# Score and maximum products on row tiles of the TensorE array, with dense rings of queries and keys

## The chip, the cores and the metric

One core of a Trainium2 chip runs the whole program. The metric is device time in microseconds (us); the program was timed three times.

## What is computed

For each of 8 blocks of 512 tokens with 256 channels, two gated layers. `xn` is the layer norm of `x`; each layer adds attention times SiLU of a feed-forward net:

```python
x = x + L0_attn(xn) * silu(L0_ffn(xn))      # 16 query heads of 16 channels on 4 key heads, ALiBi-like bias
xn = layernorm(x)
x = x + L1_attn(xn) * silu(L1_ffn(xn))      # 32 query heads of 8 channels, in pairs: a0 - lambda * a1
# both: scores = q @ k.T * scale (+ bias), causal; softmax; @ v; @ Wo
# L0_ffn: silu(x W1) * (x W3), Hadamard transform, W2 ; L1_ffn: shared expert plus top 2 of 8 experts
```

## The kernel before

The attention of a block is cut into **units** of four query heads: units 0 to 3 are layer 0, units 4 to 11 layer 1. A loop (`nc.Fori`) runs over the 8 blocks. Each engine has its instructions in an order written out by hand, with semaphores between engines; nothing is reordered by a planner.

Products of queries and keys use high and low parts stacked along the contraction, so that q and k have 48 rows in layer 0 (three times 16) and 24 in layer 1. The SyncE queue loads them from images in memory into two-slot rings, `qring` and `kring` (`ring_load`, L302 to L309). A ring has 128 rows. In layer 0 rows 0 to 47 hold the heads' 48 rows. In layer 1 the four heads of a unit lie at rows 0, 32, 64 and 96 of `kring`, and in `qring` each head has its own full-width plane that is zero outside its own 32 rows: a product over all 128 rows then gives that head's scores. The last row (`MROW`, row 127) holds ones in the keys and, in the queries, minus each query's maximum score, so that the score product (`pe_score_pack`, L410) subtracts it.

The maxima come one unit ahead: `pe_max_pack` (L387) multiplies queries by keys for unit u + 1, a product with an identity and a causal mask in bf16 (L391) adds the mask to the diagonal block, `dve_maxima` (L645) reduces each row. `pe_max_turn` (L397) transposes the 16 maxima of each token, ScalarE copies them (L543), and `max_row` (L323) writes them by DMA into row 127 of the ring. Two PSUM banks (`MX`) take the maximum products and two (`SC`) the scores; pack n waits until the reader of pack n - 2 is done.

A unit has 11 **packs**: keys tile 0 for each of 4 heads (512 columns), tile 1 for each (384), tile 2 for two heads at once (512), twice, and tile 3 for all four (512). On TensorE pack i is: score product of unit u, maximum product or products of unit u + 1, mask product; in layer 0 also an up product of the feed-forward net between them (`pe_up_between`, L338). ScalarE takes the exponent of each score pack (L554), GpSimd cuts the diagonal blocks (L1358; in layer 0 L665 and L668, with L656 on VectorE), and `pe_pv` (L425) multiplies by the values: the four heads write 17 columns each, at output partitions 0, 32, 64 and 96. In layer 1 the value product of tile 0 (pv0) stands after pack 5, that of tile 1 (pv1) after pack 10, then come the turn of the maxima (L397), twelve up products, and the value products of tiles 2 and 3 together.

Units 4 to 10 have score and maximum packs side by side; so have units 0 to 2. Units 3 and 11 have scores alone. The maxima of unit 4 are made in the front of layer 1 among up products, those of unit 0 of the next block at the end of the iteration among down products (`pe_down`, L486). The order on TensorE in a unit:

```python
for i in range(PACKS):
    pe_score_pack(pe, u, i)
    if more:
        pe_max_pack(pe, u + 1, i)
...
    if i == (7, 5)[layer_of(u)]:
        pe_pv(pe, u, 0)
...
pe_pv(pe, u, 1)
```

## Time and profile before

| what | value |
|---|---|
| three runs | 2509.87, 2512.74 and 2505.23 us, median 2509.87 us |
| profiled execution, first to last instruction (its span) | 2511.7 us |
| TensorE (PE) busy | 2154.0 us, 86% of the span |
| weight loads (PEld) | 1470.1 us, 59% |
| VectorE (DVE) | 1466.3 us, 58% |
| ScalarE (ACT) | 926.7 us, 37% |
| GpSimd (POOL) | 750.2 us, 30% |
| mean granted TensorE clock | 0.943 of full speed |

The profiled execution has no separate time beside its span; the span lies inside the range of the three runs, 1.8 us above their median. Busy time is the union of the instructions of an engine. The ends of matmuls are modelled, and include the way through the array, so start-to-start distances say more than durations. In a timeline row `x4` stands for four instructions merged; what stands in brackets is the idle time of the engine before the row, and who ended it.

### The profile page before, as it was taken

How to read it: one execution, taken by the hardware profiler on the slowest of the kernel's cores; microseconds unless marked ns; L12 is line 12 of the kernel's file. 1: busy time of each engine (PE TensorE's matmuls, PEld its weight loads, DVE VectorE, ACT ScalarE, POOL GpSimd, SP SyncE). 2: the span in 40 equal slices, each digit the busy share in tenths (PEclk: the TensorE clock that was granted, in tenths of full speed). 3: DMA queues.
4: the chain of work that ended last, by engine and by line, in shares of the span. 5: the costliest groups of instructions: out<-in, count | busy, mean ns of one | idle time of the engine just before them, and what ended most of it. 6: DMA issues, size and time to landing. Idle time of an engine off the chain costs nothing. (4 is left out here: it accounts for less than half of the span.)

```text
span 2511.7 us, 34684 instructions
## 1 busy us (share of the span) xinstructions
PE 2154.0 (86%) x12379; PEld 1470.1 (59%) x12476; DVE 1466.3 (58%) x2657; ACT 926.7 (37%) x1826; POOL 750.2 (30%) x916
## 2 busy tenths in 40 slices
PE   2379997899978999799988999789997899979998
PEld 1247565565656656475564756557565665646556
DVE  4475664656565664656647566465655566465564
ACT  2242541425323352324514245142532335233352
POOL 2342331423223331323314233142322333132331
PEclk7599998999989999899999999899998999989999
DMA  6723322253311532215232342224331253221522
GB/s 216 247 62 127 114 92 49 64 158 91 90 42 52 178 88 77 55 57 171 73 91 59 107 138 80 56 68 146 104 90 36 58 177 87 80 55 48 172 81 81
DMA packets 108131, 245.94 MB, mean 98 GB/s; under 512 B 17188, under 2 KB 27956, under 8 KB 107676
## 3 DMA queue, kind: packets, MB, share of 16 engines
q1 hardware_dynamic: 93676, 199.46, 26.5%
q0 software_dynamic: 14256, 43.94, 6.0%
q8 instruction: 111, 1.82, 0.3%
q14 instruction: 88, 0.72, 0.1%
HBM read 182.75 MB, written 59.79 MB: 97 GB/s over the span
## 5 line engine op out<-in xcount | busy, mean ns | idle before, releaser
L645 DVE TENSOR_REDUCE nmax<-bank 128x1 f32<-128x512 f32 (+3 forms) x1067 | 661.4, 639 | 457.5 <-PE bank L391 445.9
L554 ACT ACTIVATE probs<-bank 128x512 f32<-128x512 f32 (+1 forms) x1056 | 578.0, 560 | 515.5 <-PE bank L410 490.1
L338 PE MATMUL bank<-xnT,upring 128*128 128x512 f32 (+1 forms) x2220 | 626.7, 405 | 22.2 <-DMA upring<-up_img 22.2
L410 PE MATMUL bank<-qring,kring 128*128 128x512 f32 (+1 forms) x1056 | 493.1, 470 | 91.1 <-issue 47.4
L387 PE MATMUL bank<-kring,qring 127*128 127x512 f32 (+3 forms) x1552 | 480.0, 362 | 87.7 <-DMA kring<-k_img 50.1
L338 PEld LDWEIGHTS bank<-xnT,upring 128*128 128x128 f32 x2220 | 402.6, 193 | 98.8 <-issue 38.3
L387 PEld LDWEIGHTS bank<-kring,qring 127*128 127x128 f32 x1552 | 287.2, 202 | 162.3 <-DVE nmax L645 79.3
L410 PEld LDWEIGHTS bank<-qring,kring 128*128 128x128 f32 x1056 | 216.7, 206 | 216.8 <-issue 108.5
L486 PE MATMUL bank<-wdown,hbuf 128*128 128x256 f32 x1408 | 342.0, 393 | 0.0
L425 PE MATMUL bank<-probs,v 128*17 128x512 f32 (+3 forms) x3072 | 271.6, 449 | 64.9 <-DVE probs L656 40.4
L1358 POOL TENSOR_SCALAR_AFFINE_SELECT probs<-probs 128x512 f32<-128x512 f32 x256 | 162.5, 635 | 518.0 <-ACT probs L554 516.4
L486 PEld LDWEIGHTS bank<-wdown,hbuf 128*128 128x128 f32 x1408 | 268.0, 197 | 34.8 <-issue 1.7
L665 POOL TENSOR_SCALAR_AFFINE_SELECT probs<-probs 128x256 f32<-128x256 f32 x128 | 67.5, 527 | 663.9 <-ACT probs L554 663.8
L673 DVE SCALAR_TENSOR_TENSOR hbuf<-tb,bank 128x512 f32<-128x512 f32 x176 | 120.5, 685 | 224.3 <-ACT tb L564 223.4
L391 PE MATMUL bank<-causal_bf,ident_bf 128*128 128x128 bf16 (+1 forms) x970 | 245.2, 253 | 0.0
L656 DVE SCALAR_TENSOR_TENSOR probs<-probs,shared 128x512 f32<-128x512 f32 (+3 forms) x256 | 210.6, 848 | 49.7 <-ACT probs L554 48.9
L668 POOL TENSOR_TENSOR probs<-probs,shared 128x1024 f32<-128x1024 f32 (+3 forms) x128 | 211.8, 1654 | 10.7
L391 PEld LDWEIGHTS bank<-causal_bf,ident_bf 128*128 128x128 bf16 x1067 | 108.6, 102 | 178.6 <-issue 152.4
L564 ACT ACTIVATE tb<-bank 128x512 f32<-128x512 f32 x176 | 105.3, 599 | 151.3 <-PE bank L338 151.3
L425 PEld LDWEIGHTS bank<-probs,v 128*17 128x17 f32 x3072 | 61.4, 96 | 148.8 <-issue 56.0
L681 DVE SCALAR_TENSOR_TENSOR hbuf<-hbuf,bank 128x512 f32<-128x512 f32 x176 | 120.4, 684 | 33.0 <-PE bank L338 21.6
L1317 POOL TENSOR_TENSOR hbuf<-hbuf,gring 128x512 f32<-128x512 f32 x88 | 112.7, 1280 | 48.4 <-DMA gring<-gate_img 40.3
(118 smaller groups left out, 1540.1 us busy)
## 6 DMA issues: line engine op xcount, KB each, us to landing
upring<-up_img SPq DMA_DIRECT2D x179, 512.0 KB, 4.0
q_img<-probs SPq DMA_DIRECT2D x102, 256.0 KB, 3.9
qring<-q_img SPq DMA_DIRECT2D x256, 64.0 KB, 1.9
kring<-k_img SPq DMA_DIRECT2D x64, 256.0 KB, 3.1
qring<-q_img SPq DMA_DIRECT2D x34, 384.0 KB, 5.3
k_img<-probs SPq DMA_DIRECT2D x48, 256.0 KB, 4.9
up_img<-hbuf POOLq DMA_DIRECT2D x22, 512.0 KB, 4.6
gring<-gate_img POOLq DMA_DIRECT2D x32, 256.0 KB, 3.7
```

The costliest lines, as they stand in the source:

```text
L338: last = nc.tensor.matmul(out_ap, part_a(a, pa, k), part_b(b, pb, k), start=(n == 0), stop=(n == len(steps) - 1))
L387: nc.tensor.matmul(bk[:, (g - g0) * w:(g - g0 + 1) * w], qring[l][0:MROW, s, g, qt * P:(qt + 1) * P], kring[l][0:MROW, s, 0:w], start=True ...
L391: nc.tensor.matmul(diag, ident_bf[:], causal_bf[:, 0:heads, :], start=False, stop=True, skip_group_check=True).then_inc(s_mp[k], 1)
L410: nc.tensor.matmul(SC[n % 2][:, 0:heads * w].rearrange("p (g n) -> p g n", g=heads), kring[l][:, s, kt * P:(kt + 1) * P], qring[l][:, s, g ...
L425: last = nc.tensor.matmul(PV[32 * g:32 * g + DV + 1, kt * P:T], v[l][:, kt, hv, :], probs[:, kt % 2, g, 0:T - P * kt], start=(kt == 0), st ...
L486: last = nc.tensor.matmul(FB[tt // 2][:, (tt % 2) * C:(tt % 2 + 1) * C], hbuf[:, j, tt * P:(tt + 1) * P], wdown[l][:, j, :], start=(j == 0 ...
L554: nc.scalar.activation(probs[:, kt % 2, g0:g0 + heads, 0:w], SC[n % 2][:, 0:heads * w].rearrange("p (g n) -> p g n", g=heads), ACT.Exp, sc ...
L645: nc.vector.tensor_reduce(nmax[:, u % 2, g0:g0 + heads, qt], MX[n % 2][:, 0:heads * w].rearrange("p (g n) -> p g n", g=heads), AX.X, ALU.m ...
L656: nc.vector.scalar_tensor_tensor(pr, pr, BIG, estrip[:, g, 0:w], ALU.min, ALU.mult).then_inc(s_pm, 1)
L668: nc.gpsimd.tensor_tensor(pr[:, :, 0:w], pr[:, :, 0:w], estrip[:, 2:4, 0:w], ALU.mult).then_inc(s_pm2, 1)
L673: nc.vector.scalar_tensor_tensor(hbuf[:, layer_tile(j)[1], :], tb[:], 1.0, FB[0][:], ALU.add, ALU.mult).then_inc(s_gu, 1)
L1358: nc.gpsimd.affine_select(pr, pr, [[0, G4], [1, P]], ALU.is_ge, 0.0, base=0, channel_multiplier=-1).then_inc(s_pm, 1)
```

## The change

Nothing is computed otherwise; products move to other rows of the array.

- **Layer 0**: `qring[0]` and `kring[0]` lose their slot dimension. Slot 0 lies at rows 0 to 48, slot 1 at rows 64 to 112; the maximum sits in row 48 of the slot. A score product of unit u uses the 49 rows of its slot, a maximum product of unit u + 1 the 48 of the other one.
- **Layer 1**: `qring[1]` is one plane, head g at rows 32 g to 32 g + 24, without the zeros. A product takes the 24 or 25 rows of one head, so packs hold one head each: 12 steps rather than 11 packs. Steps 0 to 3 are key tile 0 (512 columns), steps 4 to 7 tiles 1 and 3 of one head (384 and 128 columns, two products in one bank), steps 8 to 11 tile 2 (256). The maximum product beside the score of head g is that of head (g + 2) mod 4. Steps 4 to 7 take two reductions each on VectorE.
- The value products of layer 1 come in three steps: pv0 after step 6, pv1 (tiles 1 and 3) after step 10 and so ahead of step 11, tile 2 last.
- Ring loads of layer 1 are one DMA of 128 rows for the queries in place of four of 32 rows. Three memsets of rings in the set-up go.
- The mask product (128 rows of the array) and all up, down and value products stay as they were.

```diff
-MROW = P - 1
 PACKS = 11
+STEPS_OF = (11, 12)
+HROWS = 32
+KROWS = (48, 24)
 
 SCORE_PACKS = [(0, g, 1) for g in range(4)] + [(1, g, 1) for g in range(4)] + [(2, 0, 2), (2, 2, 2), (3, 0, 4)]
 MAX_PACKS = [(3, g, 1) for g in range(4)] + [(2, g, 1) for g in range(4)] + [(1, 0, 2), (1, 2, 2), (0, 0, 4)]
 PACKS_TO = (4, 8, 10, 11)
+
+PARTS_1 = (((0, 0),), ((1, 0), (3, 384)), ((2, 0),))
+
+MAX_PARTS_1 = (((3, 0),), ((2, 0), (0, 384)), ((1, 0),))
...
+def score_base(u):
+    return sum(STEPS_OF[layer_of(i)] for i in range(u))
+
+
+def pv_base(u):
+    return sum((NT, len(PARTS_1))[layer_of(i)] for i in range(u))
+
+
+def max_base(u):
+    return sum(STEPS_OF[layer_of(i)] for i in range(1, u))
+
+
+def max_head(i):
+    return (i + 2) % G4
...
-        qring = [sb("qring0", [P, 2, G4, T], F32R), sb("qring1", [P, 2, G4, T], F32R)]
-        kring = [sb("kring0", [P, 2, T], F32R), sb("kring1", [P, 2, T], F32R)]
+        qring = [sb("qring0", [P, G4, T], F32R), sb("qring1", [P, 2, T], F32R)]
+        kring = [sb("kring0", [P, T], F32R), sb("kring1", [P, 2, T], F32R)]
...
-                sp.dma_start(qring[0][0:48, s, :, :].bitcast(F32),
+                sp.dma_start(qring[0][64 * s:64 * s + 48, :, :].bitcast(F32),
                              q_img[0][4 * w:4 * w + 4].rearrange("g r n -> r g n")).then_inc(done, 16)
-                sp.dma_start(kring[0][0:48, s, :].bitcast(F32), k_img[0][w]).then_inc(done, 16)
+                sp.dma_start(kring[0][64 * s:64 * s + 48, :].bitcast(F32), k_img[0][w]).then_inc(done, 16)
-                for g in range(G4):
-                    sp.dma_start(qring[1][32 * g:32 * g + 32, s, g, :].bitcast(F32), q_img[1][4 * w + g]).then_inc(done, 16)
+                sp.dma_start(qring[1][:, s, :].bitcast(F32),
+                             q_img[1][4 * w:4 * w + 4].rearrange("g r n -> (g r) n")).then_inc(done, 16)
...
-            sp.dma_start(qring[layer_of(u)][MROW:MROW + 1, u % 2, :, :].rearrange("a g (t n) -> a (g t) n", t=NT)
-                         .bitcast(F32), mneg[:].bitcast(F32)).then_inc(s_mrow[k], 16)
+            if layer_of(u) == 0:
+                row = 64 * (u % 2) + KROWS[0]
+                sp.dma_start(qring[0][row:row + 1, :, :].rearrange("a g (t n) -> a (g t) n", t=NT)
+                             .bitcast(F32), mneg[:].bitcast(F32)).then_inc(s_mrow[k], 16)
+            else:
+                sp.dma_start(qring[1][KROWS[1]:P:HROWS, u % 2, :].bitcast(F32), mneg[:].bitcast(F32)).then_inc(s_mrow[k], 16)
...
-            n = PACKS * before + i
-            qt, g0, heads = MAX_PACKS[i]
-            w = P * (qt + 1)
+            n = max_base(u) + i
             if n >= 2:
                 pe.wait_ge(s_mr[k], n - 1)
             bk = MX[n % 2]
-            for g in range(g0, g0 + heads):
-                nc.tensor.matmul(bk[:, (g - g0) * w:(g - g0 + 1) * w], qring[l][0:MROW, s, g, qt * P:(qt + 1) * P],
-                                 kring[l][0:MROW, s, 0:w], start=True, stop=True)
-
-            diag = bk[:, 0:heads * w].rearrange("p (g n) -> p g n", g=heads)[:, :, qt * P:w]
-            nc.tensor.matmul(diag, ident_bf[:], causal_bf[:, 0:heads, :], start=False, stop=True,
-                             skip_group_check=True).then_inc(s_mp[k], 1)
+            if l == 0:
+                qt, g0, heads = MAX_PACKS[i]
+                w = P * (qt + 1)
+                rows = slice(64 * s, 64 * s + KROWS[0])
+                for g in range(g0, g0 + heads):
+                    nc.tensor.matmul(bk[:, (g - g0) * w:(g - g0 + 1) * w], qring[0][rows, g, qt * P:(qt + 1) * P],
+                                     kring[0][rows, 0:w], start=True, stop=True)
+                diag = bk[:, 0:heads * w].rearrange("p (g n) -> p g n", g=heads)[:, :, qt * P:w]
+                last = nc.tensor.matmul(diag, ident_bf[:], causal_bf[:, 0:heads, :], start=False, stop=True,
+                                        skip_group_check=True)
+            else:
+
+                rows = slice(HROWS * max_head(i), HROWS * max_head(i) + KROWS[1])
+                parts = MAX_PARTS_1[i // G4]
+                for qt, at in parts:
+                    nc.tensor.matmul(bk[:, at:at + P * (qt + 1)], qring[1][rows, s, qt * P:(qt + 1) * P],
+                                     kring[1][rows, s, 0:P * (qt + 1)], start=True, stop=True)
+                diag = parts[0][0] * P
+                last = nc.tensor.matmul(bk[:, diag:diag + len(parts) * P], ident_bf[:], causal_bf[:, 0:len(parts), :],
+                                        start=False, stop=True, skip_group_check=True)
+            last.then_inc(s_mp[k], 1)
...
-
-            nc.tensor.matmul(SC[n % 2][:, 0:heads * w].rearrange("p (g n) -> p g n", g=heads),
-                             kring[l][:, s, kt * P:(kt + 1) * P],
-                             qring[l][:, s, g0:g0 + heads, kt * P:T], start=True, stop=True).then_inc(s_sc, 1)
-
-        def pe_pv(pe, u, kt):
+            if l == 0:
+                kt, g0, heads = SCORE_PACKS[i]
+                w = T - P * kt
+                rows = slice(64 * s, 64 * s + KROWS[0] + 1)
+                last = nc.tensor.matmul(SC[n % 2][:, 0:heads * w].rearrange("p (g n) -> p g n", g=heads),
+                                        kring[0][rows, kt * P:(kt + 1) * P],
+                                        qring[0][rows, g0:g0 + heads, kt * P:T], start=True, stop=True)
+            else:
+                g = i % G4
+                rows = slice(HROWS * g, HROWS * g + KROWS[1] + 1)
+                for kt, at in PARTS_1[i // G4]:
+                    last = nc.tensor.matmul(SC[n % 2][:, at:at + T - P * kt], kring[1][rows, s, kt * P:(kt + 1) * P],
+                                            qring[1][rows, s, kt * P:T], start=True, stop=True)
+            last.then_inc(s_sc, 1)
...
-                pe.wait_ge(s_pm, 8 * U0[1] + 4 * (u - U0[1]) + kt + 1)
+                pe.wait_ge(s_pm, 8 * U0[1] + NT * (u - U0[1]) + (1, 3, 4)[step])
+                parts = PARTS_1[step]
-            for g in range(G4):
-                hv = u if l == 0 else 2 * (u - U0[1]) + g // 2
-                last = nc.tensor.matmul(PV[32 * g:32 * g + DV + 1, kt * P:T], v[l][:, kt, hv, :],
-                                        probs[:, kt % 2, g, 0:T - P * kt], start=(kt == 0),
-                                        stop=(kt == NT - 1), skip_group_check=True)
+            for kt, at in parts:
+                for g in range(G4):
+                    hv = u if l == 0 else 2 * (u - U0[1]) + g // 2
+                    last = nc.tensor.matmul(PV[32 * g:32 * g + DV + 1, kt * P:T], v[l][:, kt, hv, :],
+                                            probs[:, n % 2, g, at:at + T - P * kt], start=(kt == 0),
+                                            stop=(kt == (3, 2)[l]), skip_group_check=True)
...
+                step, g0, heads = i // G4, i % G4, 1
+                w = (T, T, 2 * P)[step]
...
+            if layer_of(u) == 0:
+                qt, g0, heads = MAX_PACKS[i]
+                last = nc.vector.tensor_reduce(nmax[:, u % 2, g0:g0 + heads, qt],
+                                               MX[n % 2][:, 0:heads * P * (qt + 1)].rearrange("p (g n) -> p g n", g=heads),
+                                               AX.X, ALU.max, negate=True)
+            else:
+                for qt, at in MAX_PARTS_1[i // G4]:
+                    last = nc.vector.tensor_reduce(nmax[:, u % 2, max_head(i), qt:qt + 1],
+                                                   MX[n % 2][:, at:at + P * (qt + 1)], AX.X, ALU.max, negate=True)
+            last.then_inc(s_mr[k], 1)
...
-                sp.wait_ge(s_qz, 1)
-                nc.gpsimd.memset(qring[0][:].rearrange("p a g n -> p (a g n)").bitcast(F32), 0.0)
-                nc.gpsimd.memset(kring[0][:].rearrange("p a n -> p (a n)").bitcast(F32), 0.0).then_inc(s_qz, 1)
-                    if t == UP_EARLY + 6:
-                        nc.vector.memset(qring[1][:].rearrange("p a g n -> p (a g n)").bitcast(F32), 0.0)
...
-                            if i == (7, 5)[layer_of(u)]:
+                            if i == (7, 6)[layer_of(u)]:
                                 pe_pv(pe, u, 0)
+                            if layer_of(u) == 1 and i == 10:
+                                pe_pv(pe, u, 1)
-                        pe_pv(pe, u, 1)
+                        if layer_of(u) == 0:
+                            pe_pv(pe, u, 1)
...
-                        for kt in range(NT):
-                            pool.wait_ge(s_exp, PACKS * u + PACKS_TO[kt])
-                            pr = probs[:, kt % 2, :, 0:P]
+                        for step in range(len(PARTS_1)):
+                            pool.wait_ge(s_exp, score_base(u) + G4 * (step + 1))
+                            pr = probs[:, (pv_base(u) + step) % 2, :, :]
+                            for _, at in PARTS_1[step]:
+                                diag = pr[:, :, at:at + P]
+                                nc.gpsimd.affine_select(diag, diag, [[0, G4], [1, P]], ALU.is_ge, 0.0, base=0,
+                                                        channel_multiplier=-1).then_inc(s_pm, 1)
```

**Order, TensorE, end of a layer-1 unit.** `L410` (now `L455`) is the score product, `L387` (`L424`) the maximum product, `L391` (`L427`) the mask product, `L425` (`L474`) the value product, `L397` (`L434`) the turn of the maxima and `L338` (`L363`) the up products. Before, from pack 10 on:

```order
L410 MATMUL bank<-qring,kring 128x512
L387 MATMUL bank<-kring,qring 128x128 x4
L391 MATMUL bank<-causal_bf,ident_bf 128x512
L425 MATMUL bank<-probs,v 17x384 x4
L397 MATMUL bank<-ident,nmax 16x128
L338 MATMUL bank<-xnT,upring 128x512 x12
L425 MATMUL bank<-probs,v 17x256 x4
L425 MATMUL bank<-probs,v 17x128 x4
```

Now, from step 10 on:

```order
L455 MATMUL bank<-qring,kring 128x256
L424 MATMUL bank<-kring,qring 128x256
L427 MATMUL bank<-causal_bf,ident_bf 128x128
L474 MATMUL bank<-probs,v 17x384 x4
L474 MATMUL bank<-probs,v 17x128 x4
L455 MATMUL bank<-qring,kring 128x256
L424 MATMUL bank<-kring,qring 128x256
L427 MATMUL bank<-causal_bf,ident_bf 128x128
L434 MATMUL bank<-ident,nmax 16x128
L363 MATMUL bank<-xnT,upring 128x512 x12
L474 MATMUL bank<-probs,v 17x256 x4
```

The value product of tile 1 stood behind the last mask product; now it stands ahead of the last step, and takes tile 3 along, which had stood at the end of the unit.

**Order, VectorE, the same unit.** `L645` (now `L705`) reduces maxima, `L694` and `L701` (`L754`, `L761`) divide the outputs of the unit before. Before:

```order
L645 TENSOR_REDUCE nmax<-bank 128x1 x5
L694 RECIPROCAL rden<-bank 128x16
L701 TENSOR_TENSOR shared<-bank,rden 128x4x64
L645 TENSOR_REDUCE nmax<-bank 128x1 x3
L645 TENSOR_REDUCE nmax<-bank 128x2 x2
L645 TENSOR_REDUCE nmax<-bank 128x4
```

Now:

```order
L705 TENSOR_REDUCE nmax<-bank 128x1 x6
L754 RECIPROCAL rden<-bank 128x16
L761 TENSOR_TENSOR shared<-bank,rden 128x4x64
L705 TENSOR_REDUCE nmax<-bank 128x1 x10
```

Eleven reductions have become sixteen.

## Rows read from the trace of the kernel before

**Rows 1.** The page, part 1: busy time, share of the span, instructions of each engine.
```profile
PE 2154.0 (86%) x12379; PEld 1470.1 (59%) x12476; DVE 1466.3 (58%) x2657; ACT 926.7 (37%) x1826; POOL 750.2 (30%) x916
```

**Rows 2.** TensorE matmuls of one layer-1 unit (timeline: start us, us, engine, line).
```profile
932.64 0.50 PE L410 MATMUL bank<-qring,kring 128*128 128x512 f32 x1
...
933.21 0.23 PE L391 MATMUL bank<-causal_bf,ident_bf 128*128 128x128 bf16 x1
...
934.23 0.51 PE L387 MATMUL bank<-kring,qring 127*128 127x512 f32 x1
934.57 0.23 PE L391 MATMUL bank<-causal_bf,ident_bf 128*128 128x128 bf16 x1
...
936.69 1.05 PE L425 MATMUL bank<-probs,v 128*17 128x512 f32 x8
937.67 0.44 PE L410 MATMUL bank<-qring,kring 128*128 128x384 f32 x1
...
942.20 0.27 PE L397 MATMUL bank<-ident,nmax 128*16 128x128 f32 x1
...
945.22 0.84 PE L425 MATMUL bank<-probs,v 128*17 128x256 f32 x16
946.00 0.50 PE L410 MATMUL bank<-qring,kring 128*128 128x512 f32 x1
946.33 0.39 PE L338 MATMUL bank<-xnT,upring 128*128 128x512 f32 x1
946.56 0.40 PE L410 MATMUL bank<-qring,kring 128*128 128x512 f32 x1
```

**Rows 3.** VectorE in the same unit (timeline).
```profile
933.48 2.65 DVE L645 TENSOR_REDUCE nmax<-bank 128x1 f32<-128x512 f32 x4 [0.77 <-PE bank L391]
...
936.79 0.25 DVE L694 RECIPROCAL rden<-bank 128x16 f32<-128x16 f32 x1
937.07 0.42 DVE L701 TENSOR_TENSOR shared<-bank,rden 128x256 f32<-128x256 f32 x1
...
938.40 1.04 DVE L645 TENSOR_REDUCE nmax<-bank 128x1 f32<-128x384 f32 x2 [0.44 <-PE bank L391]
...
941.36 0.69 DVE L645 TENSOR_REDUCE nmax<-bank 128x4 f32<-128x512 f32 x1 [0.39 <-PE bank L391]
```

**Rows 4.** GpSimd in the same unit (timeline).
```profile
935.90 0.64 POOL L1358 TENSOR_SCALAR_AFFINE_SELECT probs<-probs 128x512 f32<-128x512 f32 x1 [5.33 <-ACT probs L554]
936.50 1.28 POOL L1317 TENSOR_TENSOR hbuf<-hbuf,gring 128x512 f32<-128x512 f32 x1
```

**Rows 5.** Reductions of layer maxima by form (groups of VectorE instructions).
```profile
L645 DVE TENSOR_REDUCE nmax<-bank 128x1 f32<-128x512 f32 x388 | 257.3, 688 | 278.8 <-PE bank L391 270.1
L645 DVE TENSOR_REDUCE nmax<-bank 128x1 f32<-128x384 f32 x388 | 208.8, 553 | 101.6 <-PE bank L391 100.3
```

**Rows 6.** TensorE waiting in layer 0 (waits: us in total, times, longest).
```profile
PE bank L425 <- DVE probs L656: 40.4, 32, 1.8
```

**Rows 7.** VectorE in layer 0, unit 1: reductions of its first four packs (timeline).
```profile
1038.38 3.14 DVE L645 TENSOR_REDUCE nmax<-bank 128x1 f32<-128x512 f32 x4 [0.78 <-PE bank L391]
```

**Rows 8.** The chain of waits late in the last iteration.
```profile
2495.55 1.35 PE bank L486 x6
```

**Rows 9.** Set-up: VectorE and ScalarE (timeline).
```profile
9.37 4.78 DVE L602 TENSOR_SCALAR xn<-xin,mv,rstd 128x256 f32<-128x256 f32 x2 [1.14 <-POOL rstd L611]
...
14.05 1.67 ACT L884 CAST wqk<-probs 128x640 fp32r<-128x640 f32 x2 [11.96 <-DMA probs<-in_w_gate]
```

**Rows 10.** Stretches by window: start:end, us, busy us of each engine (count), clock, DMA.
```profile
932.60:946.00 13.40, 13.13 (x92) 7.95 (x88) 8.61 (x17) 7.14 (x14) 4.39 (x6) 1.00 0.10 21
...
1021.60:1025.00 3.40, 1.38 (x8) 0.73 (x7) 3.40 (x3) 1.22 (x3) 3.28 (x3) 1.00 0.00 0
...
1055.70:1059.00 3.30, 1.00 (x7) 0.70 (x6) 0.20 (x2) 1.45 (x3) 0.00 (x0) 1.00 0.59 170
```

**Rows 11.** Twelve up products at the lower clock, set-up (timeline of TensorE).
```profile
67.07 5.47 PE L338 MATMUL bank<-xnT,upring 128*128 128x512 f32 x12
```

80 lines of the change are left out of this document (40 added, 40 removed).

## The prediction

> **What bounds the kernel now.** The page comes first: TensorE is busy 86% of the span, VectorE 58% [rows 1]. That share counts the way through the array, so I read a single layer-1 unit instead, of which seven in each of the 8 iterations have score and maximum products side by side (units 4 to 10): 56 in all. In the window of one such unit TensorE is busy 13.13 of 13.40 us, VectorE 8.61 [rows 10]. The timeline shows that this is closer than it looks [rows 2, 3]. The unit starts at 932.64, its maxima are turned at 942.20, 9.56 us later, and the next unit starts at 946.00, after 13.36 us. VectorE's four first reductions run in one piece, 2.65 us for four of 0.69 [rows 3, 5]. With two banks a loop binds both engines: a reduction ends (933.48 + 0.69), 0.06 later the maximum product of the pack after next starts (934.23), 0.34 later its mask product (934.57), and 0.27 later the reduction of that bank (933.21 to 933.48). That is 0.69 + 0.06 + 0.34 + 0.27 = 1.36 us for two packs, 0.68 for one. The score product is outside this loop: it is over while TensorE waits for the bank. So in these packs what the change hides is already hidden.
>
> **What a switch of tiles costs.** No row of before has a row tile. The nearest are the value products, whose four heads write at four places of the array: eight matmuls of 512 columns take 0.98 us start to start (936.69, next score product 937.67), where one such matmul after another takes 0.23 (946.33 to 946.56), so eight would take 1.84 [rows 2]. Tiles do run side by side, and I take pairs on different rows to do so too. Going back from the tiles costs: the first full matmul after them holds the array 0.33 (946.00 to 946.33) and not 0.23. I take 0.10 us a switch back to the whole array, and nothing for going into tiles. The bounds are 0, if only tiles across columns pay, and 0.20, if both directions do. The mask product still uses all 128 rows, so each step switches. The Trainium skill has a rule for this, "TensorEngine Tiling (Array Packing)", Tiling Modes, Key Properties: a change of tiling mode (not of tile) drains TensorE; it gives no price, the 0.10 of the trace agrees with it, and without it the sum would be that of rivals 2 or 3.
>
> **The change, part by part.**
>
> *Layer 1, paired units.* First reduction: 0.84 after the unit's start now; the score product's 0.23 goes beside the maximum product, a switch comes: 0.71. Steps 0 to 3: the loop is 1.36 + 0.10, so 0.73 a step, 2.92 together: 3.63. Steps 4 to 7 have two reductions each. A 384-wide one takes 0.55, a 512-wide one 0.69 [rows 5], 0.14 per 128 columns, so a 128-wide one 0.27; two of 0.55 in a row take 1.04 [rows 3], so pairs overlap by 0.07: 0.75. The products have 512 columns as before (0.34), the mask 256 (+0.05): 0.75 + 0.06 + 0.34 + 0.10 + 0.05 + 0.27 = 1.57, 0.79 a step, 3.15 for four; with 0.67 of dividing between them (0.25 + 0.42) [rows 3] that gives 7.45. Steps 8 and 9 are 256 wide: reduction 0.41, product 0.23, (0.41 + 0.06 + 0.23 + 0.10 + 0.27) / 2 = 0.54 each, so the reduction of step 10 starts at 8.53 and its mask product stood at 8.26. **Here the order bites.** Now pv1 runs while VectorE reduces the last pack, and the turn follows. In the new order pv1 comes first: 0.98 as pv0 [rows 2], because it has 512 columns, from 8.33 to 9.31. Then come the last pair (0.33, after tiles), a switch (0.10), 0.27, the reduction 0.41, and 0.15 to the turn (941.36 + 0.69 to 942.20) [rows 2, 3]: 10.57 rather than 9.56, +1.01. Behind the up products only tile 2 is left: of the 0.78 now, 0.57 is columns (0.21 being the way out), a third of it goes: -0.19. **+0.82 a unit, 56 units: +46 us.** Between pv0 and pv1 GpSimd has a mask (0.64) and weighs a tile (1.28) [rows 4], then two masks: with score 7 done by 6 that ends before 8.3, so it hides. Bounds: switch 0: 0 us for 56 units; 0.20: +1.7 a unit, +95.
>
> *Layer 0, paired units.* Units 1 and 2 have an up product behind each pack; a pack takes 0.82, since four reductions that wait for it span 3.14 us, (3.14 - 0.69) / 3 [rows 7]. The pair saves 0.23, and mask and up products are full-array, so a pack pays one switch and its score's weight load is exposed (another 0.10): nearly nothing left, and the unit then waits for VectorE's distances (40.4 us over the run) [rows 6]. I take 0 for units 1 and 2. Unit 0 runs at the lower clock, where 512 columns take twice as long: its first reduction starts 0.4 earlier, VectorE is the bound from then on: 8 x -0.4 = **-3 us**. Bounds 0 and -37 (second rival).
>
> *Maxima and scores without a partner.* 12 steps in front of layer 1 and 11 packs at the end of the iteration stand among full-array products, where the down products are on the chain that ended last [rows 8]. Nothing runs beside them, each pays a switch: 23 x 0.10 x 8 = **+18 us**. Unit 3 (8 packs) and unit 11 (6 steps) alternate scores with up products; half of them wait for ScalarE anyway: 14 x 0.10 x 8 / 2 = **+6 us**. Bounds 0 and +50.
>
> *Rings.* One query DMA in place of four: the row of maxima is written later than the ring load is issued, so SyncE gains nothing that TensorE sees. Bytes are the same. *Set-up:* a memset on GpSimd goes, which held VectorE (4.78 us for an operation of 0.7), but ScalarE waited for the weights until 14.05 anyway [rows 9]; the memset on VectorE may give back up to 3: **-2 us**, once.
>
> **Sum:** 46 - 3 + 18 + 6 - 2 = +65 us. The profiled execution has 2511.7 us, the three runs a median of 2510; on the median: **2575 us**.
>
> **Rivals.**
>
> 1. *The clock falls.* TensorE now idles more in the steps. In this trace the lower level (1.2 GHz rather than 2.4) followed stretches in which it was busy 1.38 of 3.40 us and 1.00 of 3.30, and in the unit of the same view it stayed at full speed [rows 10]. Against it: between pv0 and the up products few gaps of such a length arise; for it: two products that ran one behind the other now run at once, with nothing in the place of the second. If the up products of half the units ran at the lower level, 12 of them take 5.47 us [rows 11] and not the 3.0 between turn and value product [rows 2]: 28 x 2.5 = +70, 2645 us.
> 2. *Pairs pay, switches don't* (the other side). Decided by the switch: at about 0 layer 1 comes out even (above), and in layer 0 the scores leave TensorE's path: units 1 and 2 save 4 x 0.23 + 3 x 0.17 = 1.4 each, unit 0 at the lower clock 4 x 0.43 = 1.7, so 4.6 x 8 = 37, with 2 of set-up: 2470 us. For it: tiles that run side by side [rows 2]; against: the 0.10 there. The skill's "TensorE: Matmul & The Clock Gate", Part 3, measured four row tiles of 512 columns at 3.07 times one after the other; this kernel never has more than two in a pair, and no row here shows row tiles.
> 3. *No change.* As 2, but VectorE's waits take what layer 0 gains: 2505 us.
> 4. *Row tiles do not run side by side.* Then the first and the last step of a unit lose 0.23 each: 56 x 0.5 = +28, 2603 us; inside the range of the forecast.
>
> **How the numbers follow.** About 0.3% (7.5 us) is what a measurement of this kernel tells from no change. Forecast with rival 4: 0.44, own range 2530 to 2610. Clock: 0.16. No change: 0.16. Pairs pay: 0.24, since my loop prices a form of reduction and a switch that no row shows. The range leaves out about half of rival 2 below and half of rival 1 above: 2480 to 2640. Faster 0.24, within 0.3% 0.16, slower 0.60.
>
> **What would show it.** Right: in a layer-1 unit the score and maximum products start within 0.15 us of each other, the turn comes 10.2 to 10.9 us after the start, the unit takes about 14.2; a mask product after a 512-wide pair starts 0.4 or more after it; maxima among down products hold TensorE longer. Wrong: the pack steps of layer 1 go below 0.6 us, or the turn comes before 9.6; granted clock in layer 1 below 1.00 would be rival 1; layer-0 units shorter by over 1 us would be rival 2.

## The result and the profile after

The changed kernel takes 2916.25 us (median of four runs, 2910.39 to 2924.71) against 2507.55 us before (four runs, 2504.87 to 2512.74): a ratio of 1.1635, 95% interval 1.1608 to 1.1663. It is slower by 409 us. The forecast was 2575 us, within 2480 to 2640: the direction was right and the size six times too small.

The profiled execution spans 2917.3 us. The page of the changed kernel, busy time and granted clock by slices (tenths of full speed), against [rows 1]:

```profile
PE 2662.9 (91%) x12860; PEld 1602.1 (55%) x12860; DVE 1460.5 (50%) x2976; ACT 942.6 (32%) x1890; POOL 739.0 (25%) x914
...
PEclk7588787877879769696688876888788876969679
```

VectorE's busy time hardly moved (1466 to 1461 us) although it has 16 reductions a layer-1 unit rather than 11. TensorE's grew by 509 us, and the mean granted clock fell from 0.943 to 0.788. The next view shows where. Each window is one layer-1 unit, from the turn of its maxima to the next turn, with busy time of each engine, then the clock:

```profile
core 0: us, PE busy (x) PEld busy (x) DVE busy (x) ACT busy (x) POOL busy (x), PEclk, DMA share, GB/s
995.42:1012.86 17.44, 16.83 (x93) 9.40 (x94) 8.99 (x20) 7.25 (x15) 4.83 (x7) 0.79 0.23 77
1012.86:1032.00 19.14, 18.53 (x94) 9.81 (x94) 9.06 (x20) 7.33 (x15) 4.36 (x6) 0.68 0.23 70
1032.00:1053.02 21.02, 20.42 (x93) 10.61 (x94) 9.14 (x20) 7.34 (x15) 4.79 (x7) 0.58 0.20 63
```

Before, such a unit took 13.40 us at a clock of 1.00 [rows 10]. Now it takes 17.4, 19.1 or 21.0 us, and the length follows the clock. Yet TensorE is busy 96 or 97% of each window. In before the lower level came right behind the two stretches of [rows 10] in which TensorE was busy for less than half of the time:

```profile
1025.00:1031.80 6.80, 5.46 (x21) 3.29 (x22) 4.34 (x7) 1.19 (x2) 1.68 (x3) 0.50 0.00 0
...
1059.00:1062.60 3.60, 3.60 (x12) 1.92 (x11) 1.90 (x3) 1.94 (x5) 0.00 (x0) 0.53 0.00 0
```

In the changed kernel there is no such stretch: all that is idle in each of the three windows is 0.6 us.

The timeline of TensorE in the changed kernel, one step at each level of the clock, and what follows the last maxima:

```profile
1047.40 0.58 PE L455 MATMUL bank<-qring,kring 25*128 25x256 f32 x1
1047.41 0.57 PE L424 MATMUL bank<-kring,qring 24*128 24x256 f32 x1
1047.92 0.29 PE L427 MATMUL bank<-causal_bf,ident_bf 128*128 128x128 bf16 x1
...
1058.77 0.49 PE L455 MATMUL bank<-qring,kring 25*128 25x512 f32 x1
1058.77 0.49 PE L424 MATMUL bank<-kring,qring 24*128 24x512 f32 x1
1059.19 0.23 PE L427 MATMUL bank<-causal_bf,ident_bf 128*128 128x128 bf16 x1
1059.35 0.50 PE L455 MATMUL bank<-qring,kring 25*128 25x512 f32 x1
...
1070.38 0.37 PE L434 MATMUL bank<-ident,nmax 128*16 128x128 f32 x1 [0.61 <-DVE nmax L705]
1070.50 5.01 PE L363 MATMUL bank<-xnT,upring 128*128 128x512 f32 x12
```

Score and maximum products start together (1058.77 and 1058.77), so the row tiles do run side by side. (In the whole trace about four of five pairs start within 0.02 us, the others mostly 0.2 to 0.4 us apart, which fits a wait for a bank.) A step at full clock takes 0.58 us (1058.77 to 1059.35). After the turn twelve up products take 5.01 us, where at full clock they take 3.0.

The starts of the 97 turns of maxima in both traces cut the run into stretches. Means over the iterations, in us, with the clock in brackets:

| stretch between turns | before | after | difference over the run |
|---|---|---|---|
| unit 0 (seven of them) | 27.5 (0.73) | 25.0 (0.63) | -18 |
| unit 1 | 18.2 (1.00) | 20.7 (0.81) | +20 |
| unit 2 | 21.7 (0.93) | 27.1 (0.65) | +43 |
| unit 3, layer 0's end, front of layer 1 | 70.7 (0.99) | 74.9 (0.96) | +33 |
| units 4 to 10, each | 14.1 (0.99) | 19.1 (0.70) | +281 (56 units) |
| unit 11 and the iteration's end | 62.8 (0.96) | 68.6 (0.93) | +46 |

The sum is +405, and the spans differ by 2917.3 - 2511.7 = 405.6. The layer-1 units hold seven tenths of it.

### The profile page after: what moved, and what is told of

Same layout as the page of the kernel before. It is cut to its first block and busy times, and to the rows that moved or that the text cites. A ratio compares the mean times of both kernels' runs of the same rounds, so it can differ in the third digit from the quotient of the medians.

```text
span 2917.3 us, 35801 instructions
## 1 busy us (share of the span) xinstructions
PE 2662.9 (91%) x12860; PEld 1602.1 (55%) x12860; DVE 1460.5 (50%) x2976; ACT 942.6 (32%) x1890; POOL 739.0 (25%) x914
## 5 line engine op out<-in xcount | busy, mean ns | idle before, releaser
L609 ACT ACTIVATE probs<-bank 128x512 f32<-128x512 f32 (+2 forms) x1120 | 593.3, 538 | 724.6 <-PE bank L455 404.3
L363 PE MATMUL bank<-xnT,upring 128*128 128x512 f32 (+1 forms) x2220 | 805.7, 497 | 1.4 <-DVE hbuf L733 1.0
L705 DVE TENSOR_REDUCE nmax<-bank 128x1 f32<-128x512 f32 (+3 forms) x1024 | 461.4, 487 | 331.8 <-PE bank L427 326.6
L363 PEld LDWEIGHTS bank<-xnT,upring 128*128 128x128 f32 x2220 | 508.7, 244 | 126.0 <-issue 27.4
L424 PE MATMUL bank<-kring,qring 24*128 24x512 f32 (+3 forms) x1024 | 417.4, 451 | 0.1
L455 PE MATMUL bank<-qring,kring 25*128 25x128 f32 (+3 forms) x1024 | 411.5, 449 | 0.7
L474 PE MATMUL bank<-probs,v 128*17 128x512 f32 (+3 forms) x3072 | 365.9, 584 | 4.4 <-DVE probs L716 3.3
L455 PEld LDWEIGHTS bank<-qring,kring 25*128 25x128 f32 x1024 | 204.8, 224 | 213.4 <-issue 145.3
L448 PE MATMUL bank<-qring,kring 49*128 49x512 f32 (+1 forms) x352 | 215.4, 616 | 80.3 <-issue 46.4
L414 PE MATMUL bank<-kring,qring 48*128 48x256 f32 (+3 forms) x528 | 238.0, 508 | 55.3 <-DMA kring<-k_img 43.9
L424 PEld LDWEIGHTS bank<-kring,qring 24*128 24x128 f32 x1024 | 207.9, 226 | 42.0 <-issue 25.1
L427 PE MATMUL bank<-causal_bf,ident_bf 128*128 128x128 bf16 (+1 forms) x768 | 212.6, 277 | 0.0
```

What stands on the lines that cost most here:

```text
L363: last = nc.tensor.matmul(out_ap, part_a(a, pa, k), part_b(b, pb, k), start=(n == 0), stop=(n == len(steps) - 1))
L414: nc.tensor.matmul(bk[:, (g - g0) * w:(g - g0 + 1) * w], qring[0][rows, g, qt * P:(qt + 1) * P], kring[0][rows, 0:w], start=True, stop=True)
L424: nc.tensor.matmul(bk[:, at:at + P * (qt + 1)], qring[1][rows, s, qt * P:(qt + 1) * P], kring[1][rows, s, 0:P * (qt + 1)], start=True, sto ...
L427: last = nc.tensor.matmul(bk[:, diag:diag + len(parts) * P], ident_bf[:], causal_bf[:, 0:len(parts), :], start=False, stop=True, skip_grou ...
L448: last = nc.tensor.matmul(SC[n % 2][:, 0:heads * w].rearrange("p (g n) -> p g n", g=heads), kring[0][rows, kt * P:(kt + 1) * P], qring[0][ ...
L455: last = nc.tensor.matmul(SC[n % 2][:, at:at + T - P * kt], kring[1][rows, s, kt * P:(kt + 1) * P], qring[1][rows, s, kt * P:T], start=Tru ...
```

## The experiments

The first theory was that TensorE's clock falls because the products use few rows of the array, however busy the engine is. Its rivals: the new order of steps does it; or two products at once do it, since they fill less time than two in a row. All ratios are to the kernel before, timed beside it. Each kernel was run twice, those of experiment 11 six and twelve times.

**1. Layer 1 back on 128 rows, the new order kept.**

```diff
-rows = slice(HROWS * g, HROWS * g + KROWS[1] + 1)
+rows = slice(0, P)             # qring[1] has its zeros and its plane for each head again
...
-rows = slice(HROWS * max_head(i), HROWS * max_head(i) + KROWS[1])
+rows = slice(0, P - 1)
```

> The change with its layer-1 score and maximum products on all 128 rows again (zero-padded query ring); its twelve steps, its sixteen reductions and its early second value product stay, and so do the layer-0 row tiles. If the products on few rows make the clock fall (first theory): granted clock 1.00 in nearly all layer-1 units, a unit of 14 to 15 us rather than 17.4 to 21.0, and 2560 to 2640 us in all. If the new order of steps does it (rival): clock 0.58 to 0.79 in the units as in the change, over 2850 us.

Measured: 2661.54 us, ratio 1.0591 (1.0545 to 1.0637). Windows of two units, and the timeline around the start of the second:

```profile
941.73:956.78 15.05, 13.79 (x93) 8.80 (x94) 8.93 (x20) 7.27 (x15) 4.37 (x6) 1.00 0.32 89
956.78:971.93 15.15, 13.79 (x94) 8.80 (x94) 8.92 (x20) 7.28 (x15) 4.81 (x7) 1.00 0.29 87
```

```profile
941.73 0.27 PE L435 MATMUL bank<-ident,nmax 128*16 128x128 f32 x1 [0.61 <-DVE nmax L706]
...
945.86 0.47 PE L456 MATMUL bank<-qring,kring 128*128 128x512 f32 x1 [0.46 <-DMA qring<-mneg]
946.17 0.40 PE L425 MATMUL bank<-kring,qring 127*128 127x512 f32 x1
946.41 0.23 PE L428 MATMUL bank<-causal_bf,ident_bf 128*128 128x128 bf16 x1
946.45 0.48 PE L456 MATMUL bank<-qring,kring 128*128 128x512 f32 x1
...
956.78 0.27 PE L435 MATMUL bank<-ident,nmax 128*16 128x128 f32 x1 [0.61 <-DVE nmax L706]
```

The clock is back at 1.00 with order and reductions unchanged, so the order is not what lowers it. 255 us of the loss are gone (2916 to 2662). What stays is 1.7 us a unit over 13.4 (experiment 6). The total is 22 us above the expected range: the units take 15.0 to 15.2 us where nothing disturbs them and 15.9 on the mean of all 56 (before 14.1), and layer 0 keeps its own loss (experiment 4).

**2. The pair on the same rows.** The maximum product of head i beside the score product of head i:

```diff
 def max_head(i):
-    return (i + 2) % G4
+    return i % G4
```

> The change with the maximum product of each layer-1 step on the same rows as the score product beside it (head i mod 4 rather than two further), so the two cannot run at once. If the clock falls because a product on 25 rows counts little whatever runs beside it (first theory): the units stay at 0.58 to 0.79, the maximum product starts 0.1 to 0.25 us after the score product rather than 0.01, and the time is 2910 to 3000 us. If the clock falls because two products at once fill less time than two in a row (rival): it returns to 0.9 or more in the units, and the time falls to 2650 to 2800 us.

Measured: 3187.84 us, ratio 1.2685 (1.2601 to 1.2769), slower than expected. A window and a step at full clock:

```profile
1100.16:1125.05 24.89, 24.28 (x94) 14.03 (x94) 9.45 (x20) 7.43 (x15) 4.34 (x6) 0.57 0.19 54
```

```profile
1105.92 0.50 PE L455 MATMUL bank<-qring,kring 25*128 25x512 f32 x1
1106.27 0.40 PE L424 MATMUL bank<-kring,qring 24*128 24x512 f32 x1
1106.59 0.23 PE L427 MATMUL bank<-causal_bf,ident_bf 128*128 128x128 bf16 x1
```

The maximum product now starts 0.35 us after its neighbour, TensorE is busy 98% of the window, and the clock is lower still (0.57; on the mean of the 56 units 0.61, in the change 0.69). Running at once is therefore not what lowers it. Without it the program loses another 272 us; how much of that is the longer step and how much the clock was not taken apart.

**3 and 4. One layer alone.** The change in layer 1 alone; then in layer 0 alone, on the kernel before. The lines that differ are the change's own, for instance:

```diff
-rows = slice(64 * s, 64 * s + KROWS[0])       # 3: layer 0 as before
+rows = slice(0, P - 1)
...
-qring[l][0:MROW, s, g, qt * P:(qt + 1) * P]   # 4: layer 0 on row tiles
+qring[0][64 * s:64 * s + 48, g, qt * P:(qt + 1) * P]
```

> The change in layer 1 alone: layer 0 has its zero-padded 128-row products back. From the spans between turns I expect layer 1 to hold 56 x 5.6 us of the 409 and the rest of its part (unit 3 to 4, the end of the iteration): 2820 to 2870 us. If the low clock in layer 0 were what pulls layer 1 down, it would be under 2750.

> The kernel before with the row tiles of layer 0 alone (49 and 48 rows, base 0 and 64). If products on 49 rows lower the clock too: units 1 and 2 below 0.85 clock, 2540 to 2600 us. If only the 25-row tiles do (rival): clock as before, and, with score and maximum products side by side, 2470 to 2505 us.

Measured: layer 1 alone 2882.87 us, ratio 1.1472 (1.1356 to 1.1588); layer 0 alone 2547.32 us, 1.0136 (1.0096 to 1.0177). That is +371 and +35 us, together 406 of the 409, so the two parts add. The range for layer 1 was passed by 13 us. With layer 0 alone the clock is 0.87 in unit 1 and 0.68 in unit 2 on the mean (expected: both below 0.85), and 0.99 in the layer-1 units as in before.

**5. Tiles of 64 rows.** Two heads' rows a tile, the other head's query rows zero; still a pair at once:

```diff
-rows = slice(HROWS * g, HROWS * g + KROWS[1] + 1)
+rows = slice(64 * (g // 2), 64 * (g // 2) + 64)   # qring[1][rows, s, g % 2, ...]
```

> The change with the layer-1 row tiles made 64 rows high (two heads' rows, the other head's query rows zero), so a score and a maximum product still run at once, on 2 x 64 rows rather than 25 + 24. If the number of rows in use is what the clock goes by (first theory): 0.95 or more in the layer-1 units, a unit of 15.0 to 15.7 us, 2620 to 2700 us in all. If two products at once, or row tiles as such, make it fall (rival): clock 0.6 to 0.8 as in the change and 2850 us or more.

Measured: 2711.98 us, ratio 1.0816 (1.0674 to 1.0957), 12 us above the range. Units 6 to 10 at full clock, the pair starting together:

```profile
931.03:945.91 14.88, 13.98 (x93) 7.72 (x94) 8.98 (x20) 7.27 (x15) 4.84 (x7) 1.00 0.30 90
945.91:960.98 15.07, 14.03 (x93) 7.74 (x94) 8.99 (x20) 7.28 (x15) 4.37 (x6) 1.00 0.28 89
```

```profile
950.63 0.50 PE L455 MATMUL bank<-qring,kring 64*128 64x512 f32 x1
950.64 0.50 PE L424 MATMUL bank<-kring,qring 63*128 63x512 f32 x1
951.07 0.23 PE L427 MATMUL bank<-causal_bf,ident_bf 128*128 128x128 bf16 x1
951.23 0.50 PE L455 MATMUL bank<-qring,kring 64*128 64x512 f32 x1
```

So neither row tiles nor pairs need lower the clock: these units have the pairs and the changes between tiles and whole array of the change, with more rows in use. They do not hold it everywhere. Units 4 and 5 have 0.92 and 0.86 (experiment 1: 0.98 and 0.93), and the stretch from unit 3 to the front of layer 1, where maxima on 63 rows have no partner, has 0.94 and 76.9 us (experiment 1: 0.99 and 71.9). That stretch is the larger part of what this kernel loses against experiment 1.

This is also the clean price of a pair: at full clock a step of 512 columns takes 0.60 us on row tiles (950.63 to 951.23) and 0.59 on 128 rows (945.86 to 946.45). There the pair saves nothing; over a whole unit at full clock it saves 0.1 to 0.4 us (means of units 6 to 8 and 10: 14.8 to 15.0 against 15.1).

**6. The value product of tiles 1 and 3 back behind the last step**, on the kernel of experiment 1 and on the change itself:

```diff
-                            if layer_of(u) == 1 and i == 10:
-                                pe_pv(pe, u, 1)
...
-                        if layer_of(u) == 0:
-                            pe_pv(pe, u, 1)
+                        pe_pv(pe, u, 1)
```

> The kernel of the first run (128 rows in layer 1, new order) with the value product of tiles 1 and 3 back behind the last step, where VectorE's last reduction covers it. My forecast put +1.0 us of the order's cost in that move: the unit falls from 15.05 to 14.1 and the time from 2662 to about 2605. Rival: the sixteen reductions and the twelve steps themselves cost the 1.7 us over before's 13.38, and the unit stays at 14.7 or more, 2640 us or more.

> The change with only the value product of tiles 1 and 3 back behind the last step. With 128 rows this was worth 1.1 us a unit, 85 in all. If it is a wait of its own beside the clock: 1.0 to 2.0 us a unit less at the same clocks, 2800 to 2860 us. If the lower clock covers it (rival): over 2890 us.

Measured: 2576.86 us with 128 rows, ratio 1.0277 (1.0213 to 1.034), 28 us below what was expected; 2855.54 us on the change, 1.1402 (1.1356 to 1.1448), inside the range for a wait of its own beside the clock. One window of each:

```profile
911.08:924.97 13.89, 13.70 (x98) 8.73 (x95) 8.93 (x20) 7.27 (x15) 4.36 (x6) 1.00 0.35 97
```

```profile
1039.31:1057.62 18.31, 18.31 (x97) 9.62 (x93) 9.05 (x20) 7.33 (x15) 4.81 (x7) 0.69 0.22 72
```

At full clock the move alone cost 1.1 us a unit, and what is left over 13.38 is 0.6. On the change TensorE is busy for the whole window, and yet the clock is at 0.69, which is the lower level for six tenths of the time. The same order on 128 rows, busy 13.70 of 13.89 us, has 1.00.

**7. More work.** A useless product (bf16) on all 128 rows ahead of each layer-1 score product of the change, into the bank that the score product overwrites:

```diff
+nc.tensor.matmul(SC[n % 2][:, 0:512], ident_bf[:], causal_bf[:, 0:4, :], start=True, stop=True)
 rows = slice(HROWS * g, HROWS * g + KROWS[1] + 1)
```

> The change with one added product on all 128 rows, 512 columns, ahead of every layer-1 score product, into the bank that the score product then overwrites: useless work, 12 x 0.21 us a unit at the full clock. If too few rows in use make the clock fall (first theory): 0.95 or more in the units, about 15.4 + 2.5 = 17.9 us a unit rather than 19.1 on average, and 2820 to 2880 us: more work, less time. If the clock goes by something that full products do not mend (rival): 12 x 0.21 to 12 x 0.43 a unit on top, 3050 to 3200 us.

Measured: 2785.99 us, ratio 1.1111 (1.103 to 1.1192). Two windows, and a step:

```profile
973.48:989.97 16.49, 15.59 (x103) 7.56 (x106) 9.20 (x20) 7.44 (x15) 4.34 (x6) 1.00 0.25 81
989.97:1006.46 16.49, 15.59 (x103) 7.56 (x106) 9.20 (x20) 7.44 (x15) 4.79 (x7) 1.00 0.27 81
```

```profile
1001.83 0.38 PE L453 MATMUL bank<-causal_bf,ident_bf 128*128 128x512 bf16 x1
1002.13 0.38 PE L456 MATMUL bank<-qring,kring 25*128 25x256 f32 x1
1002.14 0.38 PE L424 MATMUL bank<-kring,qring 24*128 24x256 f32 x1
```

Twelve added products a unit make the unit 16.5 us long rather than 17.4 to 21.0, and the program 130 us faster than the change. The tiles, the pairs and the number of changes between tiles and whole array are those of the change, so none of them as such lowers the clock. It did better than expected (16.5, not 17.9 us): the unit is 1.6 us longer than the 14.9 of experiment 5, while twelve products at 0.21 us are 2.5. That part of the added work falls into waits is my reading, not tested.

**8. Both layers on 64 rows, the value product back.** Experiments 5 and 6 together, and layer 0 on tiles of 64 rows:

```diff
-rows = slice(64 * s, 64 * s + KROWS[0] + 1)
+rows = slice(64 * s, 64 * s + 64)
```

> Row tiles of 64 rows in both layers (zero padding to 64, the row of maxima in row 63 of its tile) and the value product of tiles 1 and 3 back behind the last step. If rows in use decide the clock: layer-1 units at 1.00 and 14.0 to 14.6 us, units 1 and 2 of layer 0 at 0.9 or more, 2530 to 2600 us. If layer-0 tiles of 64 rows still lower the clock where a product runs without a partner (rival): layer 0 as in the change, 2590 to 2640 us.

Measured: 2634.95 us, ratio 1.0508 (1.043 to 1.0586): the rival's range, and 58 us slower than the 128 rows of experiment 6. Units 6 to 8 and 10 take 14.0 to 14.2 us at 0.98 or 0.99, but units 4, 5 and 9 take 15.9, 17.1 and 16.0 at 0.92, 0.84 and 0.90, so 64 rows in pairs do not hold the full clock throughout. Unit 1 has 0.91, but unit 2 runs at a clock of 0.71 and the stretch from unit 3 to the front of layer 1, where maxima have no partner, takes 77.2 us.

**9. The mask products left out**, on the kernel of experiment 5, so that pair follows pair:

```diff
-last = nc.tensor.matmul(bk[:, diag:diag + len(parts) * P], ident_bf[:], causal_bf[:, 0:len(parts), :],
-                        start=False, stop=True, skip_group_check=True)
```

> The run with 64-row tiles in layer 1, without the causal mask product of the layer-1 maxima (the maximum is then taken over keys that the mask leaves out as well), so a pair is followed by a pair and nothing changes back to 128 rows between them. If the way back to the whole array costs about 0.2 us a step: from the start of a 512-wide pair to its reduction 0.48 us rather than 0.69, and 0.5 to 1.5 us less a unit, 2620 to 2690 us, VectorE's reductions being the bound. If the mask products are what still held the clock up (rival): clock under 0.9 in the units and over 2750 us.

Measured: 2685.28 us, ratio 1.0722 (1.0683 to 1.0762), inside the first range. A unit at full clock takes 14.2 to 14.4 us.

```profile
950.68 0.50 PE L452 MATMUL bank<-qring,kring 64*128 64x512 f32 x1 [0.31 <-DMA kring<-k_img]
950.69 0.50 PE L424 MATMUL bank<-kring,qring 63*128 63x512 f32 x1
951.02 0.39 PE L452 MATMUL bank<-qring,kring 64*128 64x512 f32 x1
```

A pair is followed by the next pair after 0.34 us, and by the mask product after 0.43 (950.64 to 951.07): going back to 128 rows costs about 0.09. From the mask product to the next pair 0.16 us pass (951.07 to 951.23), where on 128 rows it is 0.04 (946.41 to 946.45): going into the tiles costs 0.12. So a pair with its two changes takes 0.43 + 0.12 = 0.55 us, exactly as long as two products one behind the other on 128 rows (945.86 to 946.41). The clock of the 56 units is 0.91 on the mean, against 0.97 in experiment 5, and several fell to 0.7 to 0.9, so the full-height mask products did help to hold it; neither expectation had this alone.

**10. Layer 0: few rows, or waits?** First the filler of experiment 7 in layer 0 (512 columns, on the kernel of experiment 4), which did not settle it:

```diff
+if l == 0:
+    nc.tensor.matmul(SC[n % 2][:, 0:512], ident_bf[:], causal_bf[:, 0:4, :], start=True, stop=True)
```

> The run with layer-0 row tiles alone, and one useless product on all 128 rows, 512 columns, ahead of each layer-0 score product. If rows in use decide the clock in layer 0 too (first theory): 1.00 in units 1 and 2, which take about 20 and 22 us; the total is within 2530 to 2560 us, since 11 x 0.21 us a unit go back into it. If not (rival): clock 0.87 and 0.68 as without it, and 2570 to 2620 us.

Measured: 2589 us, ratio 1.0338 (1.028 to 1.0395), unit 1 at 0.96 and unit 2 at 0.75 of the clock. The clock rose by 0.07 to 0.09, short of the 1.00 of the first theory, and the time is in the rival's range: 42 us slower than without the added products. Then two kernels that take the causes apart: before with its layer-0 products on rows 0 to 48 alone, both slots on the same rows, so no pair; and pairs of 64 rows.

```diff
-kring[l][:, s, kt * P:(kt + 1) * P],
-qring[l][:, s, g0:g0 + heads, kt * P:T],
+kring[l][rows, s, kt * P:(kt + 1) * P],      # rows = slice(0, (49, P)[l])
+qring[l][rows, s, g0:g0 + heads, kt * P:T],
```

> The kernel before with its layer-0 products reading rows 0 to 48 and 0 to 47 alone (row of maxima in row 48), both units' rings at the same rows, so nothing can run side by side; layer 1 as before. If few rows in use lower the clock in layer 0 too (first theory): 0.9 or less in unit 1 and 0.75 or less in unit 2, 20 and 25 us or more, and 2540 to 2600 us. If it is the wait for VectorE behind a faster pair (rival): clock and times of units 1 and 2 as in before, 2500 to 2515 us.

> The run with layer-0 row tiles alone, padded to 64 rows with zeros, so a pair uses 127 rows. If few rows in use are the cause (first theory): unit 1 at 0.95 or more and under 18.2 us, unit 2 at 0.85 or more, 2480 to 2510 us. If a pair's short time and the waits behind it are the cause (rival): unit 2 stays at 0.75 or less and 24 us, 2520 to 2550 us.

Measured: 49 rows without a pair 2646.47 us, ratio 1.0566 (1.053 to 1.0601); pairs of 64 rows 2529.68 us, 1.0099 (1.0065 to 1.0133). Units 1 and 2 of the 49-row kernel:

```profile
1085.59:1104.67 19.08, 18.90 (x102) 10.17 (x100) 13.70 (x23) 9.89 (x19) 8.27 (x8) 0.98 0.13 34
1104.67:1136.72 32.05, 28.95 (x103) 14.38 (x100) 15.52 (x28) 10.05 (x19) 7.92 (x8) 0.59 0.22 51
```

Unit 2 in before, then a step (score product to score product) at full clock with 49 rows and in before:

```profile
1051.92:1073.85 21.93, 17.36 (x103) 10.57 (x100) 15.68 (x26) 9.95 (x19) 8.39 (x8) 0.92 0.30 71
```

```profile
1089.75 0.50 PE L413 MATMUL bank<-qring,kring 49*128 49x512 f32 x1
...
1090.87 0.50 PE L413 MATMUL bank<-qring,kring 49*128 49x512 f32 x1
```

```profile
1038.46 0.39 PE L410 MATMUL bank<-qring,kring 128*128 128x512 f32 x1
...
1039.28 0.39 PE L410 MATMUL bank<-qring,kring 128*128 128x512 f32 x1
```

The total is above the expected range. This kernel has the instructions and the order of before; its layer-0 products read 49 or 48 rows rather than 128 or 127. On the means, unit 2 falls from 0.93 to 0.60 of the clock and goes from 21.7 to 31.9 us, at a busy share of 90% (before 79%); unit 1 falls from 1.00 to 0.92 and goes from 18.2 to 20.2 us. Nothing runs in pairs here, so pairs are out as the cause. But not all of the time is the clock's: at full clock a step already takes 1.12 us rather than 0.82, which is what changes between tiles and whole array look like. These changes come with the 49 rows; that they do not lower the clock is what experiment 7 shows, in layer 1. Pairs of 64 rows do not bring unit 2 back (0.73, 24.4 us), nor unit 1 (0.90, 19.5 us), against the first theory's range; the time is in the rival's. So in layer 0 the number of rows explains part of the fall only. What keeps the clock low there was not taken further apart; that two products at once leave less TensorE time filled is possible and not tested.

**11. A pair only where the clock is low anyway.** The stretch of unit 0 was shorter in every kernel with layer-0 tiles. Here the kernel before keeps its 128 rows, and only unit 0's scores (rows 64 to 127) and unit 1's maxima (rows 0 to 62) are tiles. For that, slot 0 of the layer-0 ring moves to rows 64 to 111 with the maxima in row 127, slot 1 has its maxima in row 63, and that row is cleared before unit 3:

```diff
+rows = slice(0, {1: 63, 3: P}.get(u, MROW))   # maximum products
...
+rows = slice(0 if u else 64, P)               # score products
```

> The kernel before with row tiles in one place alone: the scores of unit 0 (rows 64 to 127) beside the maxima of unit 1 (rows 0 to 62), where the clock is at its lower level anyway; every other product is on 127 or 128 rows. In all kernels with layer-0 tiles so far this stretch (from the turn of unit 0's maxima to that of unit 1's) took 24.6 to 25.1 us against 27.5. If the pair pays where the clock is low already: 24.6 to 25.2 in this stretch, units 1 and 2 as in before, 2480 to 2495 us. If unit 1 then starts at the lower clock because of it (rival): unit 1 at 0.85 or less and 20 us, 2500 to 2520 us.

And its control, the layout without any tile:

```diff
-sp.dma_start(qring[0][0:48, s, :, :].bitcast(F32),
+row = 64 * (1 - s)                            # kring likewise
+sp.dma_start(qring[0][row:row + 48, s, :, :].bitcast(F32),
```

> The kernel before with nothing changed but the rows in which the layer-0 rings keep their data: slot 0 in rows 64 to 111, slot 1 in rows 0 to 47 as now; every product on 127 or 128 rows. If the gain at the iteration's end of the version with tiles in unit 0 alone is the layout's (unit 0's keys land sooner, TensorE waits 0.9 us for them rather than 3.8): 59.5 to 61 us between the turns of unit 11 and unit 0, 27.5 in the stretch after it, and 2475 to 2495 us. If it was chance or the tiles' (rival): 62 to 63 us there, 2500 to 2512 us.

Measured: tiles in unit 0 alone 2480.26 us, ratio 0.9903 (0.9874 to 0.9932); the layout alone 2495.72 us, 0.9963 (0.9943 to 0.9984). Both are faster than before, by 1.0 and 0.4%, and the intervals do not overlap. Units 0 and 1 with the tiles, then with the layout alone:

```profile
998.33:1023.37 25.04, 17.45 (x63) 8.15 (x64) 13.00 (x21) 6.18 (x12) 7.13 (x6) 0.63 0.15 46
1023.37:1042.50 19.13, 16.76 (x102) 10.54 (x99) 14.80 (x24) 9.65 (x19) 8.49 (x8) 0.94 0.20 50
```

```profile
1002.27:1029.72 27.45, 15.84 (x64) 8.84 (x65) 15.37 (x20) 6.28 (x12) 7.08 (x6) 0.75 0.16 44
1029.72:1047.86 18.14, 15.79 (x102) 9.78 (x99) 15.16 (x25) 9.62 (x19) 8.47 (x8) 1.00 0.20 49
```

The tiles take 2.4 us off unit 0 and give 0.9 back in unit 1, so some 12 us over eight iterations are theirs; unit 1 comes out between what the two theories expected. The rest lies at the iteration's end. The first maximum product of unit 0 among the down products, in before, in the kernel with the tiles, and in the control:

```profile
981.65 0.79 PE L387 MATMUL bank<-kring,qring 127*128 127x512 f32 x1 [3.84 <-DMA kring<-k_img]
```

```profile
976.27 0.49 PE L392 MATMUL bank<-kring,qring 127*128 127x512 f32 x1 [0.91 <-DMA kring<-k_img]
```

```profile
980.21 0.50 PE L388 MATMUL bank<-kring,qring 127*128 127x512 f32 x1 [1.26 <-DMA kring<-k_img]
```

These are single instances, and the one of before is its longest. Over the eight iterations TensorE waits 2.4 to 3.8 us for the keys in before (3.1 on the mean), 0.9 to 3.3 with the tiles (1.6) and 1.2 to 2.7 in the control (1.7). That end of the iteration takes 59.6 us in both kernels' traces, 62.8 before. The medians show less: 3.2 us times eight would be 26, and the control gained 10 (its traced execution, 2487 us, is one of its faster ones). The rows 64 to 111 are not the reason by themselves: in experiment 1 unit 0's keys lie in rows 0 to 47 and the wait is 1.7 on the mean. The mean wait is 2.7 to 3.3 us in the three traces in which both slots of the layer-0 ring lie at the same rows (before, layer 1 alone, 49 rows), and 1.5 to 2.2 in all but one of the others, whose slots lie at different rows (experiment 7 has 2.9). Whether that is the cause was not tried. The kernel with tiles in unit 0 alone is the fastest of the study.

## Why the prediction was right in direction and wrong in size

- **The clock (rival 1, chance 0.16, 2645 us): this was the case, and its mechanism as well as its size were off.** The step that failed is that the sum prices all of layer 1 at the full clock, on the strength of one reading: the lower level "followed stretches in which it was busy 1.38 of 3.40 us". I took busy time for what the clock follows, looked for idle gaps, found few, and so gave the clock a low chance and let it reach only half of the units. The runs showed a granted clock of 0.69 on the mean of the 56 units at a busy share of 97%. Experiments 1 and 7 show in layer 1 that the rows in use count as well; experiments 5, 9 and 10 agree in part (64 rows hold the clock in some units and not in others). Few rows in layer 1 cost 255 us (2916 to 2662), of which 181 in the paired units (19.1 to 15.9 us each), against 70 in the rival. The rival's own argument, that two products at once leave the place of the second empty, is not the cause in layer 1 (experiment 2).
- **The direction was not luck.** The new order alone costs more than the whole forecast at the full clock (below), and it was forecast for its own reason. But the clock, which the forecast did not count, made most of the size.
- The Trainium skill ("TensorE: Matmul & The Clock Gate", Why this matters for your kernels) advises keeping TensorE busy without gaps to hold the full clock. Here that was not enough: the second window of experiment 6, busy 18.31 of 18.31 us, has a clock of 0.69.
- **Pairs run side by side: right.** Starts lie 0.00 to 0.02 us apart in four of five pairs. Rival 4 is out. It was priced at 28 us; experiment 2, in which the clock is lower as well, lost 272.
- **The switch: its sum right in kind, half in size.** I took 0.10 us on the way back and nothing on the way in; it is about 0.09 and 0.12, the upper end of my bounds. From a pair to its mask product my loop had 0.44, and it is 0.43; from the mask product to the next pair it had nothing, and it is 0.16. So a 512-wide step is as long as on 128 rows. The Trainium skill's rule that a change of tiling mode drains the engine ("TensorEngine Tiling (Array Packing)", Tiling Modes, Key Properties) is in line with both.
- **The order in layer 1: right in mechanism, mis-sized.** The term was +0.82 us a unit; without the clock it is 1.7 (15.05 to 13.4), 95 us rather than 46. From the unit's start to its turn it is 10.92 us (945.86 to 956.78); I had 10.57, before has 9.56. What I had as a gain of 0.19 behind the turn is a loss of 0.33 (3.80 to 4.13): the value product left there is short, and the next unit's first score waits for the row of maxima (0.46 us for the DMA).
- **Layer 0 at 0 and -3 us: wrong.** It is +35. In the run with layer 0 alone unit 0 gained 2.4 us an iteration (forecast 0.4), while units 1 and 2, at clocks of 0.87 and 0.68, lost 1.9 and 3.8 (in the change 2.5 and 5.4); this term had not considered the clock.
- **Maxima and scores without a partner, +24 us: the right places, too small.** The stretches with them grew by 33 and 46 us, at clocks of 0.96 and 0.93 (before 0.99 and 0.96); how much of this is the switch was not taken apart.
- Of the signs I named, "clock in layer 1 below 1.00 would be rival 1" is what the first view after showed.

## What to carry to other kernels

Before cutting a contraction's zero padding, ask what granted clock the stretch has, and how much of TensorE's time it fills with products of few rows: zeros in the other rows cost no columns, and in this kernel they held the full clock. A pair of row tiles paid here only in unit 0, where the clock was at its lower level for much of the time anyway; at the full clock, with a full-height product between every two pairs, a pair of 512 columns with its changes took as long as two products in a row. A busy share near 100% says nothing on the clock: read the clock column of the same windows beside it.
